# Edge messages by plain scatter to counting-sorted rows, read back by blocks, in place of accumulating scatters

## The reference

```python
n1, n2 = src, dst
future_in  = concatenate([x[n2], edge_attr], axis=1)
future_agg = segment_sum(_mlp(future_in, W1f, b1f, W2f, b2f), n1, num_segments=12500)
past_in    = concatenate([x[n1], edge_attr], axis=1)
past_sum   = segment_sum(_mlp(past_in, W1p, b1p, W2p, b2p), n2, num_segments=12500)
past_agg   = past_sum / maximum(counts, 1.0)[:, None]
out = _mlp(concatenate([past_agg, future_agg], axis=1), Wc1, bc1, Wc2, bc2) + x
x = _layernorm(x + out)
...
h = relu(normalized(segment_sum(x[src], dst) * deg_inv @ Wl.T + bl + x @ Wr.T))
```

## Time and profile before

| | |
|---|---|
| median of three runs | 7807.69 us |
| the profiled execution | 7803.06 us |
| its span | 7801.2 us |
| PE busy (share of the span) | 6822.2 us (87%) |
| PE loading weights | 5320.5 us (68%) |
| DVE busy | 4517.2 us (58%) |
| ACT busy | 2235.7 us (29%) |
| POOL busy | 5814.2 us (75%) |
| mean granted TensorE clock | 0.775 of full speed |

### The profile page before, as it was taken

How to read it: one execution, slowest core, us unless ns; L and a number is a source line. 1 busy time by engine, 2 the same in 40 slices (tenths; PEclk the granted TensorE clock), 3 DMA queues, 4 the chain that set the end, 5 groups by cost and what they waited for, 6 DMA issues and landing times. The chain is left out here.

```text
span 7801.2 us, 143006 instructions
## 1 busy us (share of the span) xinstructions
PE 6822.2 (87%) x40496; PEld 5320.5 (68%) x40496; DVE 4517.2 (58%) x17274; ACT 2235.7 (29%) x4908; POOL 5814.2 (75%) x4690
## 2 busy tenths in 40 slices
PE   5998889899898999998988888988899996999993
PEld 4777778787777778877877777766445554554552
DVE  5777777777777777533333333333666664666663
ACT  2222222222222222222222222224334334333333
POOL 5888888888888888888888888852677774777773
PEclk7777777767777766767677766666999996999995
DMA  4333333333333333222222222222323234232242
GB/s 130 34 34 34 34 34 34 34 34 34 34 34 33 34 34 34 31 27 28 27 27 27 27 27 27 27 58 82 78 72 77 73 74 70 74 74 72 74 72 52
DMA packets 716773, 374.08 MB, mean 48 GB/s; under 512 B 550947, under 2 KB 666947, under 8 KB 716209
## 3 DMA queue, kind: packets, MB, share of 16 engines
q0 software_dynamic: 319648, 158.18, 20.1%
q1 hardware_dynamic: 394399, 210.89, 10.7%
q10 hardware_dynamic: 2482, 2.00, 0.1%
HBM read 289.60 MB, written 81.09 MB: 48 GB/s over the span
## 5 line engine op out<-in xcount | busy, mean ns | idle before, releaser
L666 POOL DMA_INDIRECT future<-sbuf,sidx x1564 | 2496.7, 1596 | 485.3 <-issue 456.2
L652 POOL DMA_INDIRECT gbuf<-in_x_dram,gidx x1564 | 1605.4, 1026 | 484.2 <-issue 471.5
L1536 PE MATMUL bank<-at_dst,rows 128*128 128x512 bf16 x3136 | 1197.5, 382 | 0.5 <-ACT rows L1503 0.5
L1538 PE MATMUL bank<-at_dst,rows 128*128 128x512 bf16 x3136 | 1195.9, 381 | 0.0
L1503 ACT CAST rows<-bank 128x384 bf16<-128x384 f32 x1568 | 751.1, 479 | 1250.1 <-PE bank L1522 1249.4
L1390 POOL DMA_INDIRECT gb<-x,nidx x640 | 734.1, 1147 | 320.9 <-issue 161.0
L1390 POOL DMA_INDIRECT gb<-h,nidx x640 | 753.0, 1177 | 293.7 <-issue 159.4
L1428 DVE TENSOR_SCALAR at_dst<-iota,metaf 128x512 bf16<-128x512 f16 x3136 | 954.1, 355 | 2.8 <-PE bank L1538 1.1
L978 PEld LDWEIGHTS bank<-w1pe,featT 96*128 96x128 f32 x3128 | 726.7, 270 | 308.0 <-issue 307.5
L979 PE MATMUL bank<-w1px,srcT 65*128 65x128 f32 x3128 | 819.7, 356 | 0.0
L978 PE MATMUL bank<-w1pe,featT 96*128 96x128 f32 x3128 | 819.7, 356 | 0.0
(11 more groups left out here) (260 smaller groups left out, 11259.8 us busy)
## 6 DMA issues: line engine op xcount, KB each, us to landing
laneb<-lanes SPq DMA_DIRECT2D x448, 224.0 KB
gbuf<-in_x_dram,gidx POOLq DMA_INDIRECT x1564
comb<-in_edge_attr_dram SPq DMA_DIRECT2D x391, 64.0 KB
future<-sbuf,sidx POOLq DMA_INDIRECT x1564, 3.2
blkb<-blkrow SPq DMA_DIRECT2D x240, 98.0 KB
future<-zero POOLq DMA_DIRECT2D x16, 800.0 KB, 18.0
fut<-future SPq DMA_DIRECT2D x100, 125.0 KB
gb<-x,nidx POOLq DMA_INDIRECT x644, 2.9
```

The costliest lines, as they stand in the source:

```text
L652: pool.indirect_dma_start(out=gbuf[:, b, q, :], out_offset=None, in_=x[:, :], in_offset=bass.IndirectOffsetOnAxis(ap=gidx[:, b, q:q + 1], ...
L666: pool.indirect_dma_start(out=future[q][:, :], out_offset=bass.IndirectOffsetOnAxis(ap=sidx[:, b, q:q + 1], axis=0), in_=sbuf[:, b, q, :], ...
L1536: pe.matmul(psHM[i % 2][:, :], rows16[:, j % AR, t % 2, 0:2 * D], at_dst[:, t % DR, :], start=(b == 0), stop=(b == BLOCKS - 1))
L1538: pe.matmul(psL[i % 2][:, :], rows16[:, j % AR, t % 2, 2 * D:4 * D], at_dst[:, t % DR, :], start=(b == 0), stop=(b == BLOCKS - 1)).then_in ...
```

## The change

The messages are no longer summed before or in the scatter. Each message goes as a row of 65 numbers (64, and the source node as a key) by a plain indirect DMA to a place of its own in one DRAM table. The places are those of a counting sort by the source's block of 128 nodes (98 blocks), made for four parts of the edges (105, 105, 105 and 76 groups) apart. So the rows of a block in a part lie together. They are read back in **units**, one unit for each block and part, 392 in all: SP loads 640 rows (`back`, 166 KB), DVE makes a one-hot matrix of the keys against the block's 128 nodes (`one_hot`, 128x640), PE multiplies (`unit`, five products of 128 rows), DVE adds the 64x128 result to `fsums` in SBUF (`add_back`). A unit runs beside one group: units 0 to 97 in groups 110 to 207, 98 to 195 in groups 214 to 311, 196 to 266 in groups 320 to 390; units 267 to 391 run after the last group (`over_tail`). After them the largest block is worked out, and a block of the program takes the rows beyond 640 in further passes; with these inputs the largest block has 634 rows, and that block runs once with one unit.

For the places, all 391 groups now count members and have ranks; `own` and the rank products are f32. The counts start at the begins of the blocks: the set-up counts the first part's edges (32 Sign activations on ACT, 66 steps of 128x420 on DVE), and in each group of the first three parts ACT counts one block of the next part (`below`); `part_begins` turns the counts into begins at groups 105, 210 and 315. `positions` writes the scatter's index from the rank.

Gone are L934, L813, L919, L846, the two steps of `sidx`, the clears of the tables, and in the combine stage the loads, sums and transposes of the tables; there, a short chain (`fits`) works out from the counts whether all blocks fit. The past layer is one product a tile from `pastT` (97 rows), in place of two.

The core of the diff:

```diff
                     def messages(g, b):
                         dve.wait_ge(s_M, g + 1)
-                        dve.tensor_tensor(msg[:, b, :, :], psM[:, 0:TILES * D].rearrange("p (q d) -> p q d", q=TILES),
+                        if not (isinstance(g, int) and g < 2):
+                            dve.wait_ge(s_scdone, g)
+                        dve.tensor_copy(rows[:, b, :, D:RW].rearrange("p q a -> p (q a)"), col(srcm, g))
+                        dve.tensor_tensor(rows[:, b, :, 0:D], psM[:, 0:TILES * D].rearrange("p (q d) -> p q d", q=TILES),
                                           b2frow[:, :].unsqueeze(1).to_broadcast([P, TILES, D]),
                                           ALU.add).then_inc(s_msb, 1)
-                        dve.scalar_tensor_tensor(out=pick[:, b, :], in0=later[:, b, :], scalar=1.0, in1=away[:, b, :],
...
+                    def one_hot(u, b, pair):
+                        at = slice(u, u + 1) if isinstance(u, int) else bass.DynSlice(u, 1)
+                        dve.wait_ge(s_back[b], 16 * pair + 16)
+                        dve.wait_ge(s_B, u + 1)
+                        dve.scalar_tensor_tensor(out=oneb[:, b, :, :], in0=back[:, b, :, D:RW].to_broadcast([P, RT, P]),
+                                                 scalar=column[:, at],
+                                                 in1=lanes_b, op0=ALU.subtract, op1=ALU.is_equal).then_inc(s_oneb, 1)
+
+                    def add_back(u):
...
+                        v = fsums[:, bass.DynSlice(at, P)]
+                        dve.tensor_tensor(v, v, psB[D:2 * D, 0:P], ALU.add).then_inc(s_added, 1)
...
+                    def positions(k, b):
+                        dve.wait_ge(s_RK, k + 1)
...
+                        dve.tensor_scalar(sidx[:, b, :], psRk, -1.0, None, ALU.add).then_inc(s_sidx, 1)
...
-                            dve.scalar_tensor_tensor(out=equal[:, b, q, :], in0=psR[:, q * P:(q + 1) * P],
...
+                        if u is not None:
+                            one_hot(u, b, u // 2 if isinstance(u, int) else pair - BEHIND[part - 1] // 2)
                         if not (isinstance(g, int) and g == 0):
                             add_sums(g - 1)
                         if not final(g):
                             dve.wait_ge(s_X, g + 1)
                             dve.tensor_copy(gidx[:, b, :], col(src_i, g + 2)).then_inc(s_gidx, 1)
                             front(g + 1, 1 - b)
+                        if not (isinstance(g, int) and g == 0):
+                            positions(g - 1, 1 - b)
                         if ranked(1):
-                            places(g - 1)
+                            places(g - 1, 1 - b)
...
-                        if ranked(0):
-                            count_members(g, pair, b)
+                        count_members(g, pair, b, part)
...
-                        if ranked(0):
-                            own_rank(g, b)
+                        own_rank(g, b)
+                        if u is not None:
+                            add_back(u)
...
-                                out=future[q][:, :],
+                                out=table[:, :],
                                 out_offset=bass.IndirectOffsetOnAxis(ap=sidx[:, b, q:q + 1], axis=0),
-                                in_=sbuf[:, b, q, :], in_offset=None, compute_op=ALU.add).then_inc(s_sc[q], 16)
+                                in_=rows[:, b, q, :], in_offset=None).then_inc(s_sc[b], 16)
...
+                    def unit(u, b, pair):
+                        pe.wait_ge(s_oneb, u + 1)
+                        pe.wait_ge(s_added, u + 1)
+                        for t in range(RT):
+                            last = pe.matmul(psB[D:2 * D, 0:P], back[:, b, t, 0:D], oneb[:, b, t, :],
+                                             start=(t == 0), stop=(t == RT - 1))
+                        last.then_inc(s_B, 1)
...
+                        if u is not None:
+                            unit(u, b, None)
                         if not first:
                             sums(g - 1, 1 - b, ranked)
-                            equal_sums(g - 1, 1 - b)
...
-                            pe.matmul(psP[:, tile], featT[0:W + DE, b, tile], w1pe[:, :], start=True, stop=False)
-                            last = pe.matmul(psP[:, tile], srcT[:, b, tile], w1px[:, :], start=False, stop=True)
+                            last = pe.matmul(psP[:, tile], pastT[:, b, tile], w1p[:, :], start=True, stop=True)
```

More of the change, by code:

```diff
@@ L48 @@
 TABLE = PEG + SBS * POOLG
-RANKED = PEG // 2
+PART = 105
+PARTED = [PART, PART, PART, GROUPS - 3 * PART]
+UNITS = 4 * BLOCKS
+RT = 5
+RROWS = RT * P
+RW = D + 1
+REGION = PART * GROUP + RROWS
+REGION_END = [REGION * k + PARTED[k] * GROUP for k in range(4)]
+TROWS = REGION_END[3] + RROWS
+OPENS = [110, 214, 320]
+BEHIND = [110, 116, 124]
+HJ = 112
+HACT = 32
 XB = 7
@@ L79, in build @@
           Wl0, bl0, Wr0, Wl1, bl1, Wr1, out):
-    future = [nc.dram_tensor(f"future{q}", [ROWS, D], F32).ap() for q in range(TILES)]
+    table = nc.dram_tensor("table", [TROWS, RW], F32).ap()
     xT = nc.dram_tensor("xT", [D, NW], F32).ap()
@@ L763, in count_members @@
                         dve.wait_ge(s_member, k + 1)
-                        dve.tensor_tensor_scan(count[:, :], member[:, :], member[:, :], carry[:, :],
+                        dve.tensor_tensor_scan(count[:, :], member[:, :], member[:, :],
+                                               clog[:, k + part:k + part + 1] if first else count[:, GROUP - 1:GROUP],
                                                ALU.add, ALU.max).then_inc(s_count, 1)
@@ L837, in _, with unit @@
                     add_sums(GROUPS - 1)
+                    positions(GROUPS - 1, 0)
+                    def unit(u, b, pair):
+                        one_hot(u, b, pair)
+                        add_back(u)
+                    over_tail(dve, unit)
+                    largest = [rk[0:1, c:c + 1] for c in range(TILES)]
+                    nxt = srcm[0:1, 0:BLOCKS, :].rearrange("a b s -> a s b")
+                    now = starts[:, :].rearrange("a (s b) -> a s b", s=4)
+                    dve.tensor_copy(nxt[:, :, 0:BLOCKS - 1], now[:, :, 1:BLOCKS])
@@ L866, in step @@
                         act.activation(hidp[:, b, :], psP[:, :], ACT.Copy, scale=SLOPE).then_inc(s_pslope, 1)
-                    over_groups(act, step)
-                    summed(GROUPS - 1, 0)
+                        if part < 3:
+                            if not (isinstance(g, int) and g == 0):
+                                act.wait_ge(s_hist, g)
+                            below(g - PART * part if part else g, part + 1)
+                    over_groups(act, step, part_begins)
                 @block.tensor
@@ L924, in _, with step @@
+                    pe.sem_inc(s_B, 2)
                     pe.wait_ge(s_wedge, 64)
                     pe.wait_ge(s_ones, 2)
-                    def step(g, pair, b, early, ranked):
+                    def step(g, pair, b, early, ranked, part, u):
                         first = isinstance(g, int) and g == 0
-                        if not first:
-                            pe.wait_ge(s_eu, 4 * g)
-                        pe.wait_ge(s_sm, g + 1)
-                        for q in range(TILES):
-                            last = pe.transpose(psR[:, q * P:(q + 1) * P],
-                                                skey[:, b, q:q + 1].to_broadcast([P, P]), ident[:, :])
-                        last.then_inc(s_R, 1)
@@ L1086, in _ @@
                 pool.memset(acc[0:D, N:NA], 0.0)
[L1087 removed]
+                stages(None, None, None, clear_sums)
             @block.vector
```

562 lines of the change are left out of this document (354 added, 208 removed).

## The result

The changed kernel takes **9139.5 us** (four runs, 9120.3 to 9160.3) against 7805.6 us before: 1.171 times as long, 95% interval 1.169 to 1.173. The forecast was 8690 us with a range of 8000 to 9150, so the direction is right, the size is 450 us short, and the time lies at the range's upper end. Its profiled execution took 9160.31 us, with a span of 9158.5 us and a mean granted clock of 0.688 (0.775 before).

A forecast was written before the change was run, and what follows sets the result against it. POOL was taken to bound the edge stage (5025 of 7803 us); 7803 + 448 (loop) + 400 (tail) + 12 + 30 + 12 - 15 = 8690 us. Own range 8400 to 8950, whole range 8000 to 9150.

The forecast's parts named there:

- The mechanism: Edge stage: a group costs one trip round the DVE and PE chain, in place of POOL's pace.
- Which clock: PE in the edge loop: waits in every trip leave a quarter of the time at 2.4 GHz, against 43% before.
- +448: Edge loop's term in us: 5473 us for 391 groups at the mixed clock, against 5025 before.
- by rate: Edge loop: mixes fast and slow trips as 1 / (0.25/10.8 + 0.75/12.8), giving 12.24, 16.24 and 13.57 us a group.
- the second rival: PE's clock stays at 1.2 GHz: loop +826 us, tail 444, total 9110 us; chance 0.28.
- The run of PE: Edge loop: unbroken PE run of 6.9 us before the clock rose, expected to shrink to 4.4 us at 1.2 GHz.
- The unit and the ranks at 1.2 GHz: PE in the edge loop: a unit's ten records take 2.15 us, the four f32 rank products 1.8 us.
- The ranks at 2.4 GHz: PE in the edge loop: four f32 rank products take 0.9 us, half their slow price.
- The tail: After the last group: 125 units in line, 3.2 us each at a mixed clock (3.55 slow, 2.5 fast), +400 us.
- The small terms: Beginnings of parts +12 us, tail's end +30, set-up +12, combine stage -15 (between 0 and -60).
- The two layers stay: The two layers after the combine stage: no change in time.
- the signs: POOL idle by DVE's sidx, scatter near 1.0 us, add_sums idle 4 to 7 us, tail about 400, clock near 0.6.

The follow-up runs named there:

- experiments 1: Changed kernel with the unit's five products moved on PE from ahead of the rank products to behind the past layer: 8127.9 us.
- Experiment 4: Changed kernel with PE making the four f32 rank products twice in every group: 9889.6 us.
- experiment 5: Changed kernel with the unit moved behind the past layer, and the four rank products moved on PE behind the past sums: 7583.6 us.
- experiment 8: Kernel before the change with plain in place of accumulating scatters, so that messages aren't added up: 6981.0 us.
- experiment 7: Changed kernel with only the tail altered: four row buffers, two places for the product, next one-hot ahead of the last add: 8856.1 us.
- experiment 9: Changed kernel with only the four rank products moved on PE behind the past sums, the unit left in the trip: 8826.2 us.
- experiment 11: Kernel with unit and ranks moved and the pipelined tail, with own laid out by tiles: 7199.8 us, 0.923 of the kernel before.
- experiment 10: Changed kernel with own laid out by tiles, so PE reads the rank products' weights without a step: 9104.3 us.
- experiment 6: Kernel with unit and ranks moved, plus a tail with four row buffers, two product banks and next one-hot before the last add: 7290.8 us.

## Why the prediction was right, and where it fell short

- **The mechanism** was right: the serial trip through one-hot, unit, ranks, sums, add_sums and own took POOL's place as the bound (experiments 1, 4, 5, and DVE's 6.3 us of idle a group).
- **"Which clock"** is the step that failed, less by the share that it took than by what it let the share do. "I take a quarter" of the time at 2.4 GHz was said for all groups; the windows show 36% (0.68) without a unit, 26% (0.63) ranked with one, and 12% (0.56) unranked with one. Put into the forecast's own formula these shares give 12.0, 16.2 and 14.2 us, only some 60 us more in the loop, which came out 360 longer than its +448. The formula, "by rate", lets the time at 2.4 GHz shorten the trip in proportion, wherever it falls. Here are two trips in a row (5008.44 is the add_sums shown above), then the unit, ranks and sums of the first, then products of the second that DVE did not wait for:

```profile
4993.06:5008.44 15.38, 14.97 (x63) 12.36 (x63) 6.09 (x15) 3.19 (x6) 8.69 (x8) 0.50 0.17 40
5008.44:5023.83 15.39, 13.43 (x63) 11.29 (x64) 6.21 (x15) 3.19 (x6) 8.58 (x8) 0.61 0.19 40
5001.02:5008.24 7.22, 7.22 (x35) 6.66 (x35) 0.00 (x0) 0.21 (x1) 3.65 (x4) 0.50 0.17 41
5012.50:5014.40 1.90, 1.90 (x16) 1.45 (x14) 1.90 (x3) 1.56 (x4) 1.39 (x2) 1.00 0.32 64
```

```profile
5012.53 1.00 PE L1072 MATMUL bank<-w2f,hid 128*128 128x64 f32 x8
...
5016.41 2.40 PE L1080 MATMUL bank<-oneb,back 128*64 128x128 f32 x10 [1.96 <-DVE oneb L859]
```

About a fifth of the second trip was at 2.4 GHz, and it was no shorter. The upper level fell on messages and transposes, which stand beside the trip; PE finished them sooner and waited 1.96 us for the one-hot in place of 0.41. In groups 114 to 207 and 246 to 311 the past sums ran at 0.50 in every trip, and the rank products at 0.50 and 0.51 in the mean. What shortened a trip was a unit that itself ran at the upper level: 16.35 us on the mean in place of 17.43 in 32 of 93 ranked trips, and 14.3 to 15.1 in place of 15.39 in 4 of 65 unranked ones. So a group with a unit takes about the trip at 1.2 GHz, forecast at 17.2 and 14.9 us and measured at 17.01 and 15.29. With 17.2, 14.9 and the forecast's 12.24 for the groups without a unit, the loop comes within 60 us of the measured one. That is why the second rival ("clock stays at 1.2 GHz", 9110 us) comes nearest in time, though the clock was at that level all the time only in the tail.
- **The run of PE** from which the lower share was argued was misread. Before the clock rose in the earlier trace rows PE had not run for 6.9 us: it had been busy without a gap since 4490.91, behind a wait of 4.03 us, with 0.50 granted. Nor did the run shrink to 4.4 us: in the trip shown above, with a unit, it goes from 5001.02 to 5014.45, 13.4 us, with 0.50 granted for all but the last 2. The first product of that run and the window up to the rise, in the kernel before:

```profile
4490.91 0.79 PE L961 MATMUL bank<-ident,gbuf 128*64 128x128 f32 x4 [4.03 <-DMA gbuf<-in_x_dram,gidx]
4491.20:4518.40 27.20, 27.20 (x121) 23.99 (x120) 6.79 (x27) 5.63 (x11) 22.02 (x18) 0.50 0.27 24
```

- **The range** held by its breadth: the forecast's own, 8400 to 8950 us, was missed, and 9139.5 lies 10 us inside the 9150 that the second rival had put there.
- **The unit and the ranks at 1.2 GHz** were a little small: ten records 2.33 to 2.40 us for 2.15, the ranks 1.9 for 1.8. With them a ranked trip with a unit at the lower clock takes up to 17.6 us in place of 17.2, and an unranked one 15.4 in place of 14.9.
- **The ranks at 2.4 GHz**, forecast at 0.9 us, take 1.9 us there too (last section). In the groups without a unit, where 0.87 was granted in the mean while they ran, that lengthens the trip. Experiment 4 pays that price in full.
- **The tail** is the second term that was too small: 492 us for 400. It was worked out at a mixed clock of 3.2 us; the clock stood at 0.50 throughout, and 0.3 us that the profile puts down to issue lie ahead of every second one-hot. At 1.2 GHz the sum had 3.55; the row shows 3.94.
- **The small terms** came out: the three beginnings of a part cost about 5, 5 and 3 us (the trips across them are 17.6, 17.6 and 15.7 us, those near them some 12.5), the set-up 7.7 us for 12 (the edge stage's first copy of indices at 104.72 against 97.07), the combine stage 290.3 us in place of 303.7 to the layers' first gather, -13.4 for -15. The tail's end was put at 30 and adds some 10 (523.6 less the tail's 492 and the 21.5 of before).
- "The two layers stay" did not quite hold: from their first gather to the end of the span it is 2374 us in place of 2323. With the same code in the other experiments it lies between 2343 and 2376, and in experiment 8, whose layers are those of the kernel before, at 2337. Some 10 to 50 us of that stay unexplained.
- Of the signs, POOL's idle time is not put down to `sidx` by the profile, as was forecast, but to "issue", 2073 of 2110 us. The granted clock was 0.50 to 0.68 in the loop and the tail for "near 0.6"; the rest came as named.
- The Trainium skill tells, in "TensorE: Matmul & The Clock Gate", section "HAM oscillation — how this bites in real kernels", of a kernel in which each burst of products behind a wait for a DMA starts at the lowered clock. The changed kernel's tail agrees in kind, with shorter waits: 0.50 with a wait of 1.41 to 1.68 us for the one-hot in each unit, and 1.00 in experiment 7, where PE was 91% busy. The groups do not follow PE's busy time: at 93% busy the granted clock was 0.56, and at 81% busy 0.63.

## What to carry to other kernels

Where two in-order engines hand work to each other in each turn, write down the trip first: a step costs its whole duration if it stands between one engine's wait and the other's, and nothing if the same step stands in the stretch where its engine would wait anyway. Adding work to a loop is cheap or dear by its place more than by its size: the 392 units cost 1600 us where they were put, and once they and the ranks were moved and the tail was pipelined, the kernel ran faster than before the change. After a step is moved, look again for what is now queued behind it (experiment 9), and judge two such moves together, since the second may pay only after the first: the ranks' move won 313 us alone and 544 us after the unit's. And read the clock where the trip's own products run: a share of time at the upper level that falls beside the trip only makes the faster engine wait longer.

## What the runs showed of the hardware that was not expected

The four f32 rank products (98x128 weights, one column each) took the same time at both clock levels, and the cause is how their weights lay. In experiment 5 they ran with 1.00 granted. Windows of that kernel, the first within the rank products, the second within the unit, and PE's timeline:

```profile
3311.20:3313.00 1.80, 1.80 (x9) 1.80 (x9) 0.86 (x4) 0.00 (x0) 1.29 (x2) 1.00 0.43 117
...
3315.40:3317.60 2.20, 2.20 (x11) 1.97 (x10) 2.13 (x5) 1.12 (x3) 1.70 (x2) 0.50 0.19 34
```

```profile
3309.61 1.00 PE L1045 MATMUL bank<-comb,hid 128*128 128x64 f32 x8
3310.54 0.68 PE L1048 MATMUL bank<-comb,ones 128*64 128x64 f32 x8
3311.15 2.03 PE L1058 MATMUL bank<-ones,own 98*128 98x1 f32 x8
```

They take 1.89 us to the next start at 2.4 GHz, as at 1.2 GHz in the changed kernel (5003.35 to 5005.23), while the eight records of L1045 beside them take 0.93. In experiment 11, where the weights have no step:

```profile
3311.42 1.05 PE L1079 MATMUL bank<-ones,own 98*128 98x1 f32 x8
3312.34 1.10 PE L1154 MATMUL bank<-featT,wwin 97*128 97x512 f32 x2
```

0.92 us at 2.4 GHz. So at 2.4 GHz weights read with a step of four f32 elements held the products at twice the time that they take without it. At 1.2 GHz that hardly shows: without the step they take 1.73 us there to the next start (experiment 10), with it 1.88:

```profile
5010.03 1.87 PE L1049 MATMUL bank<-ones,own 98*128 98x1 f32 x8
5011.76 1.95 PE L1053 MATMUL bank<-comb,hid 128*128 128x64 f32 x8
```

And in experiment 5 the clock fell, behind the rank products, from 1.00 to 0.50 although PE had no idle time there; in experiment 11 the mean granted clock is 0.841 in place of experiment 6's 0.819. Whether the step also lowered the clock is not shown: no run tried it apart.
